# Products of the identity in TensorE's waits in both passes of the first layer's experts

## The chip, the cores and the metric

The kernel runs on one core of a Trainium2 chip. The metric is the device time of one execution in microseconds (us); lower is better. Before the change it is 2140.37 us, the median of three runs (2134.65 to 2141.48).

## What is computed

Two transformer layers, one after the other. The stage that is changed is the mixture of experts of the first layer. Each of 4096 rows of 128 numbers is given to two of eight experts, one after the other, and an expert is two small matrix products with a bias each and a relu between:

```
_L0_ffn_ref(x, gate_W, gate_b, W1, b1, W2, b2, ln_gamma, ln_beta):      # E = 8, D = 128, H = 256, TOP_K = 2
    topk_vals, topk_idx = top_k(softmax(x @ gate_W + gate_b), 2)
    boost = x
    for i in range(2):
        h  = relu(boost @ W1[e] + b1[e])          # e = topk_idx[:, :, i], 128 -> 256
        eo = h @ W2[e] + b2[e]                    # 256 -> 128
        outs.append(eo)
        if i < 1: boost = boost + 0.5 * eo
    fused = sum(topk_vals[:, :, i] * outs[i])
    return layer_norm(x + fused)
```

The rest (an attention before it; behind it a layer that trains its own weights by two gradient steps, and a second mixture of experts) is not touched.

## The kernel before

The stages run one after the other on the five engines; each opens a block of programs, one for each engine, and a barrier stands between the blocks. `experts_0(core, keep, i)` is called twice, for the first (`i = 0`) and for the second expert of each row (`i = 1`); I call the two calls **pass 1** and **pass 2**. Rows have been sorted by expert into 40 tiles of 128 slots (`SLOT_TILES`), so that all rows of a tile have one expert. All programs are written out in full, tile by tile, and run in the order written:

- GpSimd (POOL) gathers the rows of a tile from DRAM into one of eight buffers `xg` (L850). From the ninth tile on it waits for `row_ready`, until the tile that had the buffer before is finished.
- TensorE (PE) takes, in step n, three tiles: it turns the rows of tile n (`turn_rows`, L859), does the first layer of tile n-1 (`first_layer`, L868) and the second of tile n-2 (`second_layer`, L877). A product in float32 takes two instructions on PE, so that the three are 1, 4 and 4 matmul instructions with as many weight loads, 9 a tile.
- ScalarE (ACT) copies the turned rows out of PSUM (`xgT`, L922), does bias and relu of one half of the hidden layer (`hT`, L910) and copies the next tile's weights of the first layer into a ring of three (`own`, L904).
- VectorE (DVE) does the other half of the hidden layer (L934), adds the second bias (`y`, L941) and writes the finished row (L946 to L948), which SyncE (SP) stores to DRAM (L965).

PSUM buffers, `xgT` and `hT` come in pairs, so that PE may write for tile m only when tile m-2 has been read. `keep_busy(pe, bank, ident, n)` puts n products of the identity with itself into a PSUM buffer; nothing reads them. Other stages use it already (30 of them stand ahead of the projections, at 1212 us of the trace); `experts_0` does not.

Of the kernel before, what the change touches and what calls it, by code (L numbers as in the profile page):

```python
# [593 lines left out]
def keep_busy(pe, bank, ident, n):  # L594

    for _ in range(n):
        pe.transpose(bank[:, 0:P], ident[:, :], ident[:, :])
# [210 lines left out]
def experts_0(core, keep, i):  # L808
# [6 lines left out]
    w1, w2, b2, ident = (keep[k] for k in ("w1", "w2", "b2", "ident"))  # L815
# [5 lines left out]
    with ExitStack() as st:  # L821
# [4 lines left out]
        x_ps, y_ps = bank("x_ps"), bank("y_ps")  # L826
        h_ps = [[core.ps(st, f"h_ps{j}_{f}", [P, 512]) for f in range(F)] for j in range(2)]
# [7 lines left out]
        def experts_of(eng, m):  # L835

            _, four = nc.values_load_multi_w_load_instructions(
                expert[0:1, i, m:m + 4], engines=[eng.engine], min_val=0, max_val=E_0 - 1,
                skip_runtime_bounds_check_because="places_0 writes the smaller of a count and E_0 - 1")
            return four  # L840

        @block.gpsimd
        def _(pool):
            if i == 0:
                pool.wait_ge(keep["x_out"], 64)
            for n in range(SLOT_TILES):
                r = n % X_RING
                if n >= X_RING:
                    pool.wait_ge(row_ready, n - X_RING + 1)
                pool.indirect_dma_start(out=xg[r][:, :], out_offset=None, in_=table,  # L850
                                        in_offset=bass.IndirectOffsetOnAxis(ap=source[:, i, n:n + 1], axis=0)).then_inc(gathered[r], 16)

        @block.tensor
        def _(pe):
            def turn_rows(n):
                pe.wait_ge(gathered[n % X_RING], 16 * (n // X_RING + 1))
                if n >= 2:
                    pe.wait_ge(x_ready, n - 1)
                pe.transpose(x_ps[n % 2][:, 0:P], xg[n % X_RING][:, 0:D], ident[:, :]).then_inc(x_turned, 1)  # L859

            def first_layer(m):
                pe.wait_ge(own_ready, m + 1)
                pe.wait_ge(x_ready, m + 1)
                if m >= 2:
                    pe.wait_ge(hT_by_act, m - 1)
                    pe.wait_ge(hT_by_dve, m - 1)
                for f in range(F):
                    mm = pe.matmul(h_ps[m % 2][f][:, 0:P], own[m % W_RING][:, f * P:(f + 1) * P], xgT[m % 2][:, :], start=True, stop=True)  # L868
                mm.then_inc(h_done, 1)

            def second_layer(m, e):
                pe.wait_ge(hT_by_act, m + 1)
                pe.wait_ge(hT_by_dve, m + 1)
                if m >= 2:
                    pe.wait_ge(y_ready, m - 1)
                for f in range(F):
                    mm = pe.matmul(y_ps[m % 2][:, 0:D], hT[m % 2][:, f, :], w2[:, bass.ds(F * e + f, 1), :].rearrange("p a d -> p (a d)"),  # L877
                                   start=(f == 0), stop=(f == F - 1))
                mm.then_inc(y_done, 1)

            if i == 0:
                pe.wait_ge(keep["w_in"], 80)
            for n in range(STEPS):
                if live(n):
                    turn_rows(n)
                if live(n - 1):
                    first_layer(n - 1)
                if live(n - 2):
                    if (n - 2) % 4 == 0:
                        four = experts_of(pe, n - 2)  # L890
                    second_layer(n - 2, four[(n - 2) % 4])
# [1824 lines left out]
```

## Time and profile before

| | |
|---|---|
| median of three runs (not profiled) | 2140.37 us (2134.65 to 2141.48) |
| span of the profiled execution, the only time shown for it | 2178.4 us |
| pass 1 / pass 2 in the trace | 1034 to 1115 us / 1118.5 to 1191.5 us |
| TensorE busy over the span | 1866.1 us (86%) |
| mean granted TensorE clock over the span | 0.921 |

The trace counts time from the first instruction. A row of the timeline has a start, a duration, the engine, the line of the code, the operation with its output and inputs, how many instructions were merged into it, and in brackets how long the engine stood idle before it and what ended that. The granted clock is a share of full speed: 1.00 is 2.4 GHz and 0.50 is 1.2 GHz.

### The profile page before, as it was taken

How to read it: one execution, taken by the hardware profiler on the slowest of the kernel's cores; microseconds unless marked ns; L12 is line 12 of the kernel's file. 1: busy time of each engine (PE TensorE's matmuls, PEld its weight loads, DVE VectorE, ACT ScalarE, POOL GpSimd, SP SyncE). 2: the span in 40 equal slices, each digit the busy share in tenths (PEclk: the TensorE clock that was granted, in tenths of full speed). 3: DMA queues.
4: the chain of work that ended last, by engine and by line, in shares of the span. 5: the costliest groups of instructions: out<-in, count | busy, mean ns of one | idle time of the engine just before them, and what ended most of it. 6: DMA issues, size and time to landing. Idle time of an engine off the chain costs nothing. (4 is left out here: it accounts for less than half of the span.)

```text
span 2178.4 us, 35417 instructions
## 1 busy us (share of the span) xinstructions
PE 1866.1 (86%) x11556; PEld 1497.2 (69%) x11556; DVE 1597.3 (73%) x4179; ACT 1237.1 (57%) x2908; POOL 543.2 (25%) x602
## 2 busy tenths in 40 slices
PE   8999999999999999984766486999889998962772
PEld 6888888888888888873656344777667766741662
DVE  7999999999999999976546475777467765767524
ACT  6888888888888888864444363333233322440333
POOL 0111111111111111110544502444034421000472
PEclk9999999999999999996879587999999999985796
DMA  7000000000000000013554100000000000022354
GB/s 226 1 1 1 1 1 1 1 1 1 1 1 1 1 1 1 1 36 56 99 95 105 52 1 1 0 0 0 1 0 0 0 0 5 2 58 87 85 99 92
DMA packets 64893, 61.06 MB, mean 28 GB/s; under 512 B 10698, under 2 KB 54708, under 8 KB 64612
## 3 DMA queue, kind: packets, MB, share of 16 engines
q1 hardware_dynamic: 52276, 41.50, 6.5%
q0 software_dynamic: 10384, 16.59, 4.9%
q8 instruction: 82, 1.34, 0.3%
q10 hardware_dynamic: 2080, 1.05, 0.2%
q14 instruction: 71, 0.58, 0.1%
HBM read 40.12 MB, written 18.73 MB: 27 GB/s over the span
## 5 line engine op out<-in xcount | busy, mean ns | idle before, releaser
L461 DVE TENSOR_TENSOR probT<-turn_ps,probT 128x512 fp32r<-128x512 f32 x512 | 335.3, 686 | 63.3 <-ACT probT L359 63.2
L374 ACT ACTIVATE prob<-prob,negmax 128x512 f32<-128x512 f32 x512 | 375.4, 740 | 4.6 <-DVE negmax L455 4.6
L176 POOL TENSOR_TENSOR x<-x,scaled 128x512 f32<-128x512 f32 x128 | 166.8, 1303 | 802.1 <-DVE scaled L476 802.1
L455 DVE CUSTOM_DVE_ANT_0 prob<-score_ps,bias 128x512 f32<-128x512 f32 x512 | 341.2, 685 | 6.9 <-issue 1.1
L359 ACT CAST probT<-turn_ps 128x512 fp32r<-128x512 f32 x512 | 284.0, 598 | 21.7 <-PE turn_ps L259 21.7
L259 PE MATMUL turn_ps<-ident,prob 128*128 128x128 f32 x2048 | 266.2, 273 | 1.3 <-DVE probT L461 1.1
L276 PE MATMUL work_ps<-probT,val 128*128 128x512 f32 x1024 | 257.2, 393 | 0.1
L259 PEld LDWEIGHTS turn_ps<-ident,prob 128*128 128x128 f32 x2048 | 236.7, 140 | 28.2 <-DVE probT L461 3.4
L247 PE MATMUL score_ps<-k,q 64*128 64x512 f32 x1536 | 213.8, 410 | 2.4 <-DVE negmax L455 2.1
L276 PEld LDWEIGHTS work_ps<-probT,val 128*128 128x128 f32 x1024 | 187.5, 188 | 39.9 <-DVE probT L461 1.7
L247 PEld LDWEIGHTS score_ps<-k,q 64*128 64x128 f32 x1536 | 135.4, 185 | 47.3 <-issue 19.7
L1587 ACT CAST dpT_hi<-pred_ps 128x128 fp32r<-128x128 f32 x64 | 17.1, 267 | 234.1 <-PE pred_ps L1534 234.1
L291 PE MATMUL work_ps<-wo,ctxT 128*128 128x128 f32 x1024 | 146.0, 286 | 0.7 <-ACT ctxT L366 0.7
L291 PEld LDWEIGHTS work_ps<-wo,ctxT 128*128 128x128 f32 x1024 | 123.9, 191 | 26.3 <-issue 22.6
L1515 POOL TENSOR_TENSOR w<-c,vc 128x512 f32<-128x512 f32 x64 | 83.1, 1298 | 207.1 <-DVE c L1627 207.1
L366 ACT COPY ctxT<-work_ps 128x512 f32<-128x512 f32 x128 | 75.1, 587 | 84.5 <-PE work_ps L276 83.4
L374 ACT ACTIVATION_READ_ACCUMULATOR prob<-prob,negmax 128x1 f32 x512 | 106.1, 207 | 0.0
L476 DVE TENSOR_TENSOR scaled<-work_ps,inv 128x512 f32<-128x512 f32 x128 | 87.8, 686 | 2.7 <-PE work_ps L291 2.7
L1620 DVE TENSOR_TENSOR s<-u_ps,sg 128x512 f32<-128x512 f32 x64 | 44.3, 692 | 54.6 <-ACT sg L1592 54.6
L1504 POOL CAST kTs_hi<-turned_hi 128x128 fp32r (+1 forms) x64 | 45.5, 710 | 133.0 <-SPq L1474 133.0
L868 PE MATMUL h_ps<-xgT,own 128*128 128x128 f32 x320 | 60.6, 320 | 14.5 <-issue 14.5
L877 PE MATMUL y_ps<-w,hT 128*128 x320 | 60.6, 319 | 12.7 <-issue 7.2
(510 smaller groups left out, 4010.5 us busy)
## 6 DMA issues: line engine op xcount, KB each, us to landing
ew<-L_ffn_fc_weight SPq DMA_DIRECT2D x32, 256.0 KB
bias<-bias_line SPq DMA_DIRECT2D x16, 448.0 KB, 8.4
mid_rows<-row SPq DMA_DIRECT2D x40, 128.5 KB
last_rows<-row SPq DMA_DIRECT2D x40, 64.0 KB
rows_dram<-qk SPq DMA_DIRECT2D x1, 2304.0 KB, 18.5
x_rows<-x SPq DMA_DIRECT2D x4, 512.0 KB, 7.1
acc_dram<-zero POOLq DMA_DIRECT2D x1, 2048.0 KB, 16.3
out<-x SPq DMA_DIRECT2D x4, 512.0 KB
```

The costliest lines, as they stand in the source:

```text
L176: pool.tensor_tensor(mine, mine, scaled[a][:, :, :], ALU.add).then_inc(added, 1)
L247: mm = pe.matmul(score_ps[i % 2][a][:, :], q[p % 2][u][head(a), tile_of(i)], k[p % 2][v][head(a), :], start=(n == 0), stop=(n == 2))
L259: mm = pe.transpose(turn_ps[g % 2][:, tile_of(t)], prob[p % 2][a][:, t, tile_of(c)], ident[:, :])
L276: mm = pe.matmul(work[a][:, :], val[p // 2 % 2][:, c, p % 2 * 2 + a, :], probT[n][:, c, :], start=(c == 0 and n == 0), stop=(c == QT - 1 a ...
L291: mm = pe.matmul(work[1][:, tile_of(t)], ctxT[a][:, tile_of(t)], wo[:, 2 * (p % PAIRS) + a, :], start=True, stop=True)
L359: act.copy(probT[0][:, g % QT, :], turn_ps[g % 2][:, :]).then_inc(turned_hi, 1)
L366: act.copy(ctxT[a][:, :], work[a][:, :]).then_inc(ctx_ready, 1)
L374: act.activation(mine, mine, ACT.Exp, bias=negmax[p % 2][:, i, a:a + 1], scale=-1.0, accum_out=total[p % 4][:, i, a:a + 1]).then_inc(exp_d ...
L455: dve.tensor_tensor_reduce(prob[p % 2][a][:, i, :], score_ps[i % 2][a][:, :], bias[:, h, first:first + SEQ][:, ::-1], -1.0, 3.0e38, ALU.ad ...
L461: dve.tensor_tensor(probT[1][:, g % QT, :], turn_ps[g % 2][:, :], probT[0][:, g % QT, :].bitcast(F32), ALU.subtract).then_inc(turned_lo, 1)
L476: dve.tensor_tensor(scaled[a][:, :, :], work[1][:, :].rearrange("p (t d) -> p t d", t=QT), inv[p % 4][:, :, a:a + 1].to_broadcast([P, QT, ...
L1515: pool.tensor_tensor(w[r][:, :], c1[p][:, :], vc[p][:, :], ALU.mult).then_inc(w_ready, 1)
```

## The change

Three edits, all in the program of TensorE in `experts_0`: 24 products of the identity at the start of each pass, two ahead of each first layer and two ahead of each second layer. The two products write into the PSUM buffer that the layer behind them writes. For that the wait until the buffer has been read (`hT_by_act`, `hT_by_dve` of tile m-2, and `y_ready` of tile m-2) stands ahead of the products, and the wait for the operands stands behind them.

```
@@ -859,20 +859,22 @@
             def first_layer(m):
-                pe.wait_ge(own_ready, m + 1)
-                pe.wait_ge(x_ready, m + 1)
                 if m >= 2:
                     pe.wait_ge(hT_by_act, m - 1)
                     pe.wait_ge(hT_by_dve, m - 1)
+                keep_busy(pe, h_ps[m % 2][0], ident, 2)
+                pe.wait_ge(own_ready, m + 1)
+                pe.wait_ge(x_ready, m + 1)
                 for f in range(F):
                     mm = pe.matmul(h_ps[m % 2][f][:, 0:P], own[m % W_RING][:, f * P:(f + 1) * P], xgT[m % 2][:, :], start=True, stop=True)
                 mm.then_inc(h_done, 1)
 
             def second_layer(m, e):
+                if m >= 2:
+                    pe.wait_ge(y_ready, m - 1)
+                keep_busy(pe, y_ps[m % 2], ident, 2)
                 pe.wait_ge(hT_by_act, m + 1)
                 pe.wait_ge(hT_by_dve, m + 1)
-                if m >= 2:
-                    pe.wait_ge(y_ready, m - 1)
                 for f in range(F):
...
@@ -880,6 +882,7 @@
             if i == 0:
                 pe.wait_ge(keep["w_in"], 80)
+            keep_busy(pe, y_ps[0], ident, 24)
             for n in range(STEPS):
```

How TensorE's program starts in pass 1, as a difference; L597 is the product in `keep_busy`, L869 is the L868 of before, `xg_222` the first gathered tile:

```order
 L680 UNCONDITIONAL_BRANCH
 L853 UNCONDITIONAL_BRANCH
+L597 MATMUL y_ps_245<-ident 128x128 x24
 L859 MATMUL x_ps_243<-ident,xg_222 128x128
 L859 MATMUL x_ps_244<-ident,xg_223 128x128
-L868 MATMUL h_ps_0_247<-xgT_237,own_234 128x128
-L868 MATMUL h_ps_1_248<-xgT_237,own_234 128x128
+L597 MATMUL h_ps_0_247<-ident 128x128 x2
+L869 MATMUL h_ps_0_247<-xgT_237,own_234 128x128
+L869 MATMUL h_ps_1_248<-xgT_237,own_234 128x128
```

The 24 products stand ahead of the turn of the first tile. One step in the steady part of pass 1 (turn of the sixth tile, first layer of the fifth, second of the fourth), with its waits, on TensorE before. In the names of the semaphores, `bias_in0_91` is `x_ready`, `bias_in1_92` `own_ready`, `bias_in3_94` and `bias_in4_95` are `hT_by_act` and `hT_by_dve`, and `bias_in6_97` is `y_ready`:

```order
L859 MATMUL x_ps_244<-ident,xg_227 128x128 [waits bias_in0_91,gathered5_265]
L868 MATMUL h_ps_0_247<-xgT_237,own_235 128x128 [waits bias_in3_94,bias_in4_95,bias_in0_91,bias_in1_92]
L868 MATMUL h_ps_1_248<-xgT_237,own_235 128x128
L877 ISA [waits bias_in6_97,bias_in4_95,bias_in3_94]
L877 MATMUL y_ps_246<-w_114,hT_240 128x128
L877 ISA
L877 MATMUL y_ps_246<-w_114,hT_240 128x128
```

and the same step after the change:

```order
L859 MATMUL x_ps_244<-ident,xg_227 128x128 [waits bias_in0_91,gathered5_265]
L597 MATMUL h_ps_0_247<-ident 128x128 [waits bias_in4_95,bias_in3_94]
L597 MATMUL h_ps_0_247<-ident 128x128
L869 MATMUL h_ps_0_247<-xgT_237,own_235 128x128 [waits bias_in0_91,bias_in1_92]
L869 MATMUL h_ps_1_248<-xgT_237,own_235 128x128
L597 MATMUL y_ps_246<-ident 128x128 [waits bias_in6_97]
L597 MATMUL y_ps_246<-ident 128x128
L879 ISA [waits bias_in4_95,bias_in3_94]
L879 MATMUL y_ps_246<-w_114,hT_240 128x128
L879 ISA
L879 MATMUL y_ps_246<-w_114,hT_240 128x128
```

Each layer has two products ahead of it, and the waits are shared out between the products and the layer. The other engines' programs stay as they are.

## Rows read from the trace of the kernel before

**Rows 1.** The page: span, and granted clock of TensorE in 40 slices, in tenths

```profile
span 2178.4 us, 35417 instructions
PEclk9999999999999999996879587999999999985796
```

**Rows 2.** Windows: stretch and length, busy us and instructions by engine, clock, DMA share, GB/s

```profile
1034.00:1115.00 81.00, 60.70 (x360) 54.22 (x360) 46.31 (x200) 36.90 (x120) 38.03 (x40) 0.81 0.60 96
1118.50:1191.50 73.00, 53.86 (x360) 48.25 (x360) 37.22 (x120) 36.42 (x120) 37.91 (x40) 0.88 0.44 108
...
1183.00:1190.00 7.00, 6.59 (x55) 6.15 (x53) 5.78 (x21) 4.56 (x16) 0.95 (x1) 1.00 0.40 84
1107.50:1112.40 4.90, 4.74 (x22) 4.75 (x23) 2.44 (x11) 1.27 (x4) 0.00 (x0) 0.50 0.43 137
```

**Rows 3.** Timeline, TensorE at the end of pass 2: two turns, one tile apart

```profile
1183.98 0.27 PE L859 MATMUL x_ps<-ident,xg 128*128 128x128 f32 x1
...
1184.98 0.27 PE L859 MATMUL x_ps<-ident,xg 128*128 128x128 f32 x1
```

**Rows 4.** Timeline, TensorE early in pass 1: two turns, one tile apart

```profile
1041.73 0.42 PE L859 MATMUL x_ps<-ident,xg 128*128 128x128 f32 x1
...
1043.65 0.42 PE L859 MATMUL x_ps<-ident,xg 128*128 128x128 f32 x1
```

**Rows 5.** Timeline, POOL: gathers in pass 2, the last row its last gather

```profile
1170.73 0.95 POOL L850 DMA_INDIRECT xg<-mid_rows,source  x1 [1.13 <-DVE row L948]
1171.98 0.94 POOL L850 DMA_INDIRECT xg<-mid_rows,source  x1 [0.30 <-issue]
...
1176.12 0.94 POOL L850 DMA_INDIRECT xg<-mid_rows,source  x1 [1.94 <-DVE row L948]
...
1183.02 0.95 POOL L850 DMA_INDIRECT xg<-mid_rows,source  x1 [2.07 <-DVE row L948]
```

**Rows 6.** Timeline, DVE: second biases of pass 2 (tiles 22, 23, 24, 31 and 40)

```profile
1165.19 0.29 DVE L941 TENSOR_TENSOR y<-y_ps,b 128x128 f32<-128x128 f32 x1 [0.53 <-remote]
...
1166.05 0.28 DVE L941 TENSOR_TENSOR y<-y_ps,b 128x128 f32<-128x128 f32 x1
...
1167.19 0.29 DVE L941 TENSOR_TENSOR y<-y_ps,b 128x128 f32<-128x128 f32 x1 [0.22 <-PE y_ps L877]
...
1179.06 0.29 DVE L941 TENSOR_TENSOR y<-y_ps,b 128x128 f32<-128x128 f32 x1 [0.89 <-PE y_ps L877]
...
1190.77 0.29 DVE L941 TENSOR_TENSOR y<-y_ps,b 128x128 f32<-128x128 f32 x1 [0.43 <-PE y_ps L877]
```

**Rows 7.** Timeline, all engines around 1144 us, weight loads left out

```profile
1142.78 0.27 PE L859 MATMUL x_ps<-ident,xg 128*128 128x128 f32 x1
...
1145.25 0.27 ACT L922 COPY xgT<-x_ps 128x128 f32<-128x128 f32 x1 [1.72 <-PE x_ps L859]
1145.33 0.29 DVE L941 TENSOR_TENSOR y<-y_ps,b 128x128 f32<-128x128 f32 x1 [2.37 <-PE y_ps L877]
...
1145.62 0.35 PE L868 MATMUL h_ps<-xgT,own 128*128 128x128 f32 x1 [1.56 <-issue]
```

**Rows 8.** Timeline, first gather and first turn of pass 1 and of pass 2

```profile
1034.36 1.13 POOL L850 DMA_INDIRECT xg<-x_rows,source  x1 [29.10 <-POOLq L680]
...
1037.19 0.45 PE L859 MATMUL x_ps<-ident,xg 128*128 128x128 f32 x1 [4.63 <-DMA xg<-x_rows,source]
...
1119.10 0.94 POOL L850 DMA_INDIRECT xg<-mid_rows,source  x1 [17.02 <-POOLq L821]
...
1121.90 0.48 PE L859 MATMUL x_ps<-ident,xg 128*128 128x128 f32 x1 [7.81 <-DMA xg<-mid_rows,source]
```

**Rows 9.** Timeline of TensorE and windows where 30 such products stand now

```profile
1212.37 6.29 PE L597 MATMUL qk_ps<-ident 128*128 128x128 f32 x30 [5.03 <-DVE projT L1284]
...
1212.00:1218.00 6.00, 5.63 (x27) 5.66 (x28) 5.25 (x21) 1.25 (x4) 4.56 (x5) 0.50 0.20 49
1218.00:1221.00 3.00, 2.18 (x12) 1.32 (x10) 2.03 (x12) 1.43 (x4) 2.39 (x3) 0.97 0.23 60
```

More of the change, by code:

```diff
@@ L861, in first_layer @@
             def first_layer(m):
-                pe.wait_ge(own_ready, m + 1)
-                pe.wait_ge(x_ready, m + 1)
                 if m >= 2:
@@ L866, in first_layer @@
                     pe.wait_ge(hT_by_dve, m - 1)
+                keep_busy(pe, h_ps[m % 2][0], ident, 2)
+                pe.wait_ge(own_ready, m + 1)
+                pe.wait_ge(x_ready, m + 1)
                 for f in range(F):
@@ L871, in second_layer @@
             def second_layer(m, e):
+                if m >= 2:
+                    pe.wait_ge(y_ready, m - 1)
+                keep_busy(pe, y_ps[m % 2], ident, 2)
                 pe.wait_ge(hT_by_act, m + 1)
                 pe.wait_ge(hT_by_dve, m + 1)
-                if m >= 2:
-                    pe.wait_ge(y_ready, m - 1)
                 for f in range(F):
@@ L882, in _ @@
                 pe.wait_ge(keep["w_in"], 80)
+            keep_busy(pe, y_ps[0], ident, 24)
             for n in range(STEPS):
```

## The prediction

> **What bounds the kernel now.** I read the page first. Its slices show the granted clock of TensorE falling from nine tenths to 6, 8, 7, 9, 5, 8 in the middle of the span, and that is where the changed stage lies [rows 1]. The windows of the two passes give the amount: the mean clock is 0.81 over the 81 us of pass 1 and 0.88 over the 73 us of pass 2 [rows 2]. There are two levels, 1.00 and 0.50, so a mean of 0.81 says that 0.19/0.50 = 38% of the time is at half clock: 30.8 us of pass 1, and 24% or 17.5 us of pass 2. That is all that a warm clock can work on.
>
> Next I read what one tile costs on each engine. At full clock TensorE turns tile after tile exactly 1.00 us apart at the end of pass 2, when no gathers run any more, and it is busy throughout: 9 instructions in 1.00 us, 0.111 us each [rows 3], [rows 2]. At half clock two turns are 1.92 us apart, 0.213 us an instruction [rows 4]. GpSimd starts a gather every 1.25 us when nothing holds it [rows 5]. So at full clock it is not TensorE that should set the pace but GpSimd, by 1.25 against 1.00; at half clock it is TensorE, with 1.92.
>
> The trace is slower than either. From tile 22 to tile 31 of pass 2, at full clock throughout, nine tiles take 1179.06 - 1165.19 = 13.87 us, 1.54 us a tile, and the steps are not even: 0.86 and 1.14 us, then a long one [rows 6]. The long one is a stand-still of three engines at once. Around 1144 us a turn that ended at 1143.05 is taken up by ScalarE only at 1145.25, VectorE starts at 1145.33 after 2.37 us of idling, and TensorE at 1145.62, with no releaser that the profile can name [rows 7]. Such a stand-still comes about every third tile while gathers run. GpSimd then idles too, 1.13 and 1.94 us for a finished row [rows 5]. I can't name its cause. It matters for another reason: the profiled span is 2178.4 us and the median run 2140.4, so 38 us of this trace aren't in the timed runs. If both passes had gone at GpSimd's pace, pass 1 would end at 1034.36 + 39 x 1.25 + 7.8 = 1090.9 us (7.8 us is the way from the last gather to the last second bias in pass 2, 1183.02 to 1190.77, [rows 8, 5, 6]) in place of 1115, and pass 2 at 1119.10 + 48.8 + 7.8 = 1175.7 in place of 1191.5: 24 + 16 = 40 us less. This agrees with the 38, so the stand-stills may be the profiler's own. It is an argument, not proof, and I work out both readings.
>
> **The change part by part.** It removes nothing. It adds 2 x 24 + 2 x 40 x 4 = 368 products of the identity, each with its weight load, and puts the waits for free buffers ahead of the waits for operands. Moving the waits alone costs nothing: both sets had to be met before the layer, and they still must. No DMA, no other engine's program and no semaphore is touched; what is queued behind a product is TensorE's own next layer and turn, and behind those ScalarE and VectorE.
>
> *The price of a product.* Like a turn it is one load and one matmul with 128 columns, 0.111 us at full and 0.213 at half clock [rows 3, 4]. The 30 products that stand elsewhere took 6.29 us, most of them at half clock, 0.21 us each [rows 9]. That is the same.
>
> *The start of a pass.* 24 x 0.213 = 5.1 us from the moment at which the pass begins, which I put at GpSimd's first gather: until 1039.5 in pass 1 and 1124.2 in pass 2. The first rows are there at 1037.19 and 1121.90 [rows 8]. The turn is late by 2.3 us in each pass, 4.6 together; if TensorE starts half a microsecond sooner, 3.6.
>
> *The clock.* Do such products raise it? The 30 products begin at half clock with the engine idle for 5.03 us before, and nothing else runs on TensorE beside them; the window to 1218 shows 0.50, the one behind it 0.97 [rows 9]. So they do, and 24 of them should bring full clock at or soon after the first turn. With them TensorE also has little idle time left, so I expect it to stay.
> The Trainium skill speaks against this: its page "TensorE: Matmul & The Clock Gate", part 4, says that full clock does not engage for transpose mode, which is not counted as work. By that rule no clock would be gained and the sum would be that of the fourth case below; the rows just named disagree.
>
> *The pace.* With four products a tile TensorE needs 13 x 0.111 = 1.44 us at full clock. That is above GpSimd's 1.25, above the fast steps of 0.86 to 1.14, and below 1.92. What that is worth depends on the reading.
>
> Reading 1, the stand-stills are not in the timed runs. The pace goes from GpSimd's 1.25 to TensorE's 1.44. Pass 1 ends at 1039.5 + 40 x 1.44 + 0.9 (last second layer to bias) = 1098.0 against 1090.9, pass 2 at 1182.7 against 1175.7: **+14.1 us**, start included.
>
> Reading 2, they are. Tiles at half clock: (30.8 - 3.2)/1.92 = 14 in pass 1 and (17.5 - 3.4)/1.92 = 7 in pass 2, the idle time before the first turn taken off. 59 tiles are at full clock, of them 8 behind the last gather. The other 51 make 17 groups of three. The two fast steps of a group grow from a mean of 1.00 to 1.44, +0.88. In the long one I let two products vanish in the stand-still and two lie behind it, +0.22 (ends: nothing, and 0.44). Groups: 17 x 1.10 = +18.7. The eight last tiles: 7 x 0.44 = +3.1. Starts: +4.6. Tiles at half clock join the groups, whose pace is then 1.54 + 0.37 = 1.91, so 1.92 becomes 1.91: nothing. Only the four tiles at the end of pass 1, at half clock without gathers [rows 2], gain 4 x 0.48 = -1.9. Sum: **+24.5 us**.
>
> I take a value between them, nearer to the first since it explains the 38 us: +18 us, 2140.4 + 18 = **2158 us**.
>
> **The rivals.**
> *The products vanish in the waits, and the clock brings as much as they cost.* For it: in reading 2 TensorE idles 25% of the passes (60.7 us busy of 81, [rows 2]), and if a stand-still lasts until a fixed event and the ring of eight buffers sets the pace, added work in front of it is free. Against it: the fast steps run with TensorE busy without a gap. It leaves the starts (+4.6), the eight tiles (+3.1) and a third of the half-clock tiles' gain (-7 x 0.38 = -2.7): +5, 2145, within 0.3%.
> *Faster, the clock pays.* If the products are hidden and every tile goes at the full-clock pace of 1.54, then the 21 half-clock tiles alone gain 0.38 each, -8.0. The most is the whole difference of the paces: from the first turn to the end, less about 5 us for one tile's way through the engines, pass 1 takes (1115 - 1037.2 - 5)/39 = 1.87 us a tile and pass 2 (1191.5 - 1121.9 - 5)/39 = 1.66, which at 1.54 gives 39 x (0.33 + 0.12) = -17.6; the starts give back 4.6. That is 2127 us. It decides if the timed runs before hold a pace above 1.44 a tile, which is the point from which four products are cheaper than the half clock. Against it stands the 38 us reading, by which that pace is 1.25.
> *Slower still, the clock isn't held.* If products of the identity don't count, the 21 half-clock tiles take 13 x 0.213 = 2.77 in place of 1.92: +17.9 on top of the groups' cost, 2140 + 24.5 + 17.9 = 2183 us. Against it: rows 9.
>
> **How the numbers follow.** Chances: slower by my sums 0.63, balanced 0.18, faster 0.15, much slower 0.04. My case's own range is 2147 to 2170. For the range I reach down towards the faster case and a little above reading 2: 2131 to 2171, which leaves out the fourth case and about half of the faster one. A measurement of this kernel tells 0.3%, or 6.4 us, from no change. Faster than that: 0.15; within: 0.18; slower: 0.67.
>
> **What would show it.** In the trace after: 24 products at the start of a pass ending about 2 us behind the landing of the first rows; granted clock 1.00 from about 1040 us to the end of pass 1 and likewise in pass 2 (if 0.8 as before, the clock step is wrong); turns 1.44 us apart wherever nothing stands still, 13 instructions between them; GpSimd waiting for rows more often than before. The span of the passes could shrink while the timed runs grow, if the stand-stills are the profiler's: the forecast is of the timed runs. I am wrong if the median run before had TensorE at half clock for long, or if the fast steps stay at 1.0 to 1.2 us, which would say that products cost less than 0.111 us beside real work.

## The result, and the profile after

The changed kernel takes 2143.59 us, the median of 20 runs (2138.71 to 2147.03), against 2136.81 us (2132.53 to 2142.37, 20 runs) for the kernel before on the same chip. The ratio is 1.003, with a 95% interval of 1.0022 to 1.0038: 6.4 us slower, with an interval of 4.7 to 8.1 (the two medians are 6.8 us apart). The sign was forecast, the 18 us were not.

The page of the changed kernel, with the lines that answer to [rows 1] and the row of busy times (engine, busy us, share of the span, instructions):

```profile
span 2142.2 us, 36152 instructions
PE 1870.7 (87%) x11924; PEld 1514.3 (71%) x11924; DVE 1598.8 (75%) x4179; ACT 1237.6 (58%) x2908; POOL 544.1 (25%) x602
PEclk9999999999999999997799798999999999985796
```

TensorE's program has 368 more matmuls than that of before (11556). The profiled execution itself took 2144.22 us, 2.0 us more than its span. By the same 2 us an execution whose span is 2178.4 us takes about 2180 us, which no timed run of the kernel before comes near. I took a second profile of that kernel (first experiment), with a span of 2137.7 us, and compare with that one from here on.

TensorE at the start of pass 1 (start, duration, engine, line, operation, count, idle time before and its releaser) and GpSimd's first gather, which answer to [rows 8]:

```profile
1036.44 4.45 PE L597 MATMUL y_ps<-ident 128*128 128x128 f32 x24 [1.07 <-PEq L680]
1037.18 1.13 POOL L850 DMA_INDIRECT xg<-x_rows,source  x1 [29.10 <-POOLq L680]
1040.73 0.27 PE L859 MATMUL x_ps<-ident,xg 128*128 128x128 f32 x1
```

The 24 products begin 0.74 us before the gather and end at 1040.9, 3.7 us behind its start. The first turn is 3.55 us behind the gather in place of 2.83 [rows 8]. What comes next is quicker, since the clock has risen inside the products. Windows of 6 us, with columns as in [rows 2]:

```profile
1034.00:1040.00 6.00, 4.93 (x39) 4.77 (x37) 1.15 (x6) 0.80 (x2) 2.21 (x3) 0.51 0.05 12
1040.00:1046.00 6.00, 5.45 (x48) 5.03 (x47) 2.08 (x8) 3.34 (x11) 4.61 (x5) 1.00 0.25 56
1052.00:1058.00 6.00, 6.00 (x57) 6.00 (x56) 4.94 (x23) 3.84 (x14) 4.48 (x6) 1.00 0.69 139
1082.00:1088.00 6.00, 6.00 (x57) 6.00 (x56) 4.74 (x21) 4.16 (x14) 4.17 (x5) 1.00 0.87 90
```

The granted clock is 0.51 until 1040 and 1.00 from there on, and in the steady part TensorE has no idle time left: 6.00 of 6.00 us. Two of its turns in that part, and two of GpSimd's gathers:

```profile
1072.83 0.27 PE L859 MATMUL x_ps<-ident,xg 128*128 128x128 f32 x1
...
1074.27 0.27 PE L859 MATMUL x_ps<-ident,xg 128*128 128x128 f32 x1
```

```profile
1072.91 0.94 POOL L850 DMA_INDIRECT xg<-x_rows,source  x1 [0.49 <-DVE row L951]
1074.35 0.94 POOL L850 DMA_INDIRECT xg<-x_rows,source  x1 [0.50 <-DVE row L951]
```

A tile takes 1.44 us, 13 x 0.111, and GpSimd now stands idle half a microsecond ahead of each gather until a row is finished (0.30 us stands there also when it waits for nothing, [rows 5]). So TensorE sets the pace, as forecast. At the end of pass 1 it doesn't:

```profile
1092.85 0.33 PE L859 MATMUL x_ps<-ident,xg 128*128 128x128 f32 x1 [0.76 <-DMA xg<-x_rows,source]
1096.18 0.33 PE L859 MATMUL x_ps<-ident,xg 128*128 128x128 f32 x1 [1.67 <-DMA xg<-x_rows,source]
```

These two turns are 3.33 us apart, and the second waits for a gather to land. The same happens before, and longer. The clock stays at 1.00 through this wait:

```profile
1094.00:1096.00 2.00, 0.51 (x5) 0.32 (x3) 1.07 (x5) 0.66 (x2) 0.00 (x0) 1.00 0.51 66
```

The table gives both passes in the two traces. A pass is counted from its first gather to its last second bias; both kernels have 40 tiles in each.

| | before (second profile) | after |
|---|---|---|
| first gather to first second bias, pass 1 / 2 | 7.74 / 7.59 us | 7.18 / 7.04 us |
| pace of second biases, tiles 1 to 32 of pass 1 | 1.34 us | 1.44 us |
| last eight steps of pass 1 | 16.69 us | 14.71 us |
| pass 1 | 66.05 us | 66.63 us |
| pace of second biases, pass 2 | 1.30 us | 1.45 us |
| pass 2 | 58.19 us | 63.53 us |

Pass 1 grows by 0.6 us and pass 2 by 5.3, together 5.9 us, beside 6.4 timed. (The spans differ by 4.5 us. With the same code, the first gather comes anywhere from 1034 to 1037 us in the traces from here on, and what follows pass 2 takes from 967 to 975 us; in these two traces 974.1 and 970.0. So I use the lengths of the passes.)

### The profile page after: what moved, and what is told of

Its sections match the earlier page's. It is cut to its first block and busy times, and to the rows that moved or that the text cites. A ratio compares the mean times of both kernels' runs of the same rounds, so it can differ in the third digit from the quotient of the medians.

```text
span 2142.2 us, 36152 instructions
## 1 busy us (share of the span) xinstructions
PE 1870.7 (87%) x11924; PEld 1514.3 (71%) x11924; DVE 1598.8 (75%) x4179; ACT 1237.6 (58%) x2908; POOL 544.1 (25%) x602
## 5 line engine op out<-in xcount | busy, mean ns | idle before, releaser
L1558 PEld LDWEIGHTS dwp_ps<-dp,h 128*128 128x128 f32 x512 | 67.1, 191 | 5.5
L1566 PE MATMUL pred_ps<-proj,hT 128*128 128x128 f32 x512 | 67.8, 276 | 1.3 <-ACT hT L1604 1.3
```

## The experiments

Kernels of one set ran on one chip. The median of before is 2140.20 us in the first set (the first four below), 2135.95 us in the second (the next four) and 2140.37 us in the third. "Before" and "after" name the two kernels. Lengths of passes come from the one profiled execution of each kernel, ratios from the timed runs.

**The kernel before, profiled again.** No edit. It asks whether the stand-stills of [rows 7] are in an ordinary execution.

> The kernel before, unchanged, once more, for a second trace of it. The stand-still theory (the stand-stills of the first trace belong to that one execution and not to the kernel) expects no stand-stills, gathers 1.25 us apart, a span of 2132 to 2138 us that lies about 2 us below its own time, and the ratio 1.000. The clock theory (the timed runs, too, go at half clock for long) expects granted clock of about 0.81 and 0.88 in the two passes again and tiles of 1.92 us in the middle of them.

Measured: 2139.72 us, ratio 0.9999 (0.9987 to 1.0011), span 2137.7 us. No stand-still of three engines is left in the passes. GpSimd's gathers run 1.25 us apart through all of pass 2 (1105.45 to 1154.44 us, 40 gathers). The clock is at half only for the first tiles of a pass and in one stretch of pass 1; its mean over the passes is 0.89 and 0.93, where the first trace had 0.81 and 0.88 [rows 2]. Windows:

```profile
1034.00:1040.00 6.00, 2.34 (x9) 1.85 (x10) 0.35 (x1) 1.84 (x6) 4.78 (x5) 0.50 0.21 46
...
1052.00:1058.00 6.00, 6.00 (x48) 5.45 (x47) 5.12 (x23) 4.06 (x14) 4.48 (x6) 1.00 0.83 139
```

```profile
1084.00:1090.00 6.00, 4.04 (x26) 3.37 (x27) 2.25 (x10) 2.54 (x8) 1.39 (x2) 0.96 1.03 67
1090.00:1092.00 2.00, 0.58 (x3) 0.28 (x2) 1.07 (x5) 0.54 (x2) 0.00 (x0) 0.50 0.66 75
```

That stretch is new to me. TensorE works 0.58 of 2 us there, although the last gather was issued at 1085.48. Its turns, and the two of GpSimd's gathers that they belong to (the 37th was issued at 1080.24, the 38th at 1082.26 and the 40th at 1085.48):

```profile
1080.24 0.94 POOL L850 DMA_INDIRECT xg<-x_rows,source  x1 [0.30 <-issue]
1082.26 0.94 POOL L850 DMA_INDIRECT xg<-x_rows,source  x1 [1.08 <-DVE row L948]
...
1085.48 0.94 POOL L850 DMA_INDIRECT xg<-x_rows,source  x1 [1.03 <-DVE row L948]
```

```profile
1085.65 0.33 PE L859 MATMUL x_ps<-ident,xg 128*128 128x128 f32 x1 [0.16 <-DMA xg<-x_rows,source]
1088.79 0.33 PE L859 MATMUL x_ps<-ident,xg 128*128 128x128 f32 x1 [1.80 <-DMA xg<-x_rows,source]
1092.34 0.47 PE L859 MATMUL x_ps<-ident,xg 128*128 128x128 f32 x1 [1.76 <-DMA xg<-x_rows,source]
```

From the gather's issue to its turn it is 4 to 5 us for most of pass 1, then 6.7 us for the 36th, 8.55 for the 37th (1088.79 - 1080.24), and 10.1, 10.9 and 10.8 for the last three. For the 37th and the 38th TensorE stands waiting; the turns of the last two follow 2.05 and 1.92 us apart, at about its pace at half clock. VectorE's rows wait there too, for the stores of earlier rows:

```profile
1090.03 0.29 DVE L946 SCALAR_TENSOR_TENSOR row<-y,xg 128x128 f32<-128x128 f32 x1 [2.54 <-DMA mid_rows<-row]
```

**The parts of the change.** Four kernels, each the changed one with products taken out; the order of the waits stays as changed. Only the 24 at the start:

```
-                keep_busy(pe, h_ps[m % 2][0], ident, 2)
-                keep_busy(pe, y_ps[m % 2], ident, 2)
```

> Only the 24 products at the start of each pass, with the waits in the order of the change; none at the tiles. The pace theory (four products a tile lift TensorE's need from 1.00 to 1.44 us, above GpSimd's 1.25) expects 0 to 4 us less than before, -1 us likeliest: the turn of the first tile 0.7 us late, but the first tiles at full clock. The clock theory expects that the clock falls again later in the passes and the time stays as before within 3 us.

Measured: 2142.94 us, ratio 1.0011 (0.9998 to 1.0023). The first second bias is 7.15 and 6.88 us behind the gather, 0.6 to 0.7 us sooner than before, and the passes aren't shorter (67.39 and 58.43 us): from there GpSimd and the landings set the end. The pace theory's 0 to 4 us less were not measured; the ratio leaves room for 0.4 us less at most.

Only the two and two of each tile:

```
-            keep_busy(pe, y_ps[0], ident, 24)
```

> Only the two and two products at each tile, none at the start. The pace theory expects tiles 1.44 us apart from when the clock is up, and the first two or three at 13 x 0.213 = 2.8 us, so 7 to 12 us more than before, more than the whole change. The clock theory expects the time of the change less at most 2 us.

Measured: 2150.71 us, ratio 1.0048 (1.0031 to 1.0065), passes of 70.81 and 64.03 us. Without the 24, the first tiles carry their products at half clock and the first second bias comes 8.97 and 8.68 us behind the gather. Beside products in every tile, then, the 24 look worth a gain: the whole change is 1.003. The intervals of the two ratios, from two sets of runs, overlap (1.0022 to 1.0038 for the change), but the passes of the change are 4.7 us shorter together.

No products, only the moved waits (all three calls taken out):

> Only the order of the waits of the change, no product at all. Both theories expect the time of before within 1 us (ratio 1.000) and the trace of before. If it differs by 3 us or more, the order of the waits has a price of its own that the prediction set to nothing.

Measured: 2140.73 us, ratio 1.0001 (0.9989 to 1.0013). The order of the waits is worth nothing that could be measured (2.8 us at most).

**More and fewer products in a tile.** The 24 stay. One and one:

```
-                keep_busy(pe, h_ps[m % 2][0], ident, 2)
+                keep_busy(pe, h_ps[m % 2][0], ident, 1)
-                keep_busy(pe, y_ps[m % 2], ident, 2)
+                keep_busy(pe, y_ps[m % 2], ident, 1)
```

> The change with one product ahead of each layer in place of two. The pace theory expects 11 x 0.111 = 1.22 us a tile, still under GpSimd's 1.25, so that the products cost 0 to 2 us over the time of before (ratio 1.000 to 1.001). The theory that every product is paid for (about 6 us for four a tile, so half of that for two) expects 3 us more, ratio 1.0015.

Measured: 2137.14 us, ratio 0.9999 (0.9989 to 1.0008). Turns come every 1.22 us (1070.78, 1072.03 and 1073.25), with longer steps in between, as before (the passes take 66.25 and 57.95 us). TensorE needs 11 x 0.111 = 1.22, less than GpSimd's 1.25: free as far as can be measured.

Four and four, with 4 for 1 in the same lines:

> The change with four products ahead of each layer in place of two. The pace theory expects tiles 17 x 0.111 = 1.89 us apart in both passes: 39 x (1.89 - 1.30) = 23 us more in pass 2 and 31 x (1.89 - 1.34) = 17 us more in the first 32 tiles of pass 1, nothing in its last eight, so 35 to 42 us over before (ratio 1.017 to 1.020). If waits hid products, it would be clearly less, 12 to 20 us.

Measured: 2170.80 us, ratio 1.017 (1.0157 to 1.0183). Turns in the steady part:

```profile
1068.72 0.27 PE L859 MATMUL x_ps<-ident,xg 128*128 128x128 f32 x1
...
1070.59 0.27 PE L859 MATMUL x_ps<-ident,xg 128*128 128x128 f32 x1
...
1072.47 0.27 PE L859 MATMUL x_ps<-ident,xg 128*128 128x128 f32 x1
```

A tile takes 1.87 us; 17 x 0.111 is 1.89. The passes take 79.69 and 79.72 us, that is alike: at this pace the gathers land in time at the end of pass 1 too. Its last eight steps take 13.9 us, 2.8 less than before, where I had expected no difference.

**The late landings at the end of pass 1.** The eight experts' last tiles are filled up: 4096 rows are 32 tiles' worth, the stage has 40, so the last tile at least, and probably several, must be all empty slots. For an empty slot the table of rows holds 0, and its gather fetches row 0. If that one row is the cause, empty slots that fetch different rows should land in time. The edit is in the place where the table is made, on VectorE, some time ahead of the passes; an empty slot of pass 1 now fetches the row whose number is its lane:

```
             for i in range(R):
...
-                then(dve.scalar_tensor_tensor(source[:, i, :], back_ps[i][:, 0, :], float(P), line[i][:, :], ALU.mult, ALU.add))
+                if i == 0:
+                    then(dve.scalar_tensor_tensor(at[:, :], back_ps[i][:, 0, :], float(P), line[i][:, :], ALU.mult, ALU.add))
+                    then(dve.scalar_tensor_tensor(line[i][:, :], at[:, :], 0.0, token_line[:, 0:1].to_broadcast([P, K]), ALU.is_equal, ALU.mult))
+                    then(dve.tensor_tensor(source[:, i, :], at[:, :], line[i][:, :], ALU.add))
```

In the kernel before:

> The kernel before, but the empty slots of pass 1 gather the row of their own lane (0 to 127) and not row 0 all of them; two small VectorE operations more ahead of pass 1 (0.4 us). Theory of the repeated row (the last tiles of pass 1 are slow since the 128 slots of the empty tiles fetch one and the same row) expects the last eight tiles in 9 to 12 us in place of 16.7, landings of 5 us in place of 6 to 11, and 4 to 7 us less than before (ratio 0.997 to 0.998). If the tail has another cause: ratio 1.000 and the tail of 16.7 us again.

Measured: 2131.13 us, ratio 0.9977 (0.9968 to 0.9985), which is faster than both kernels. Pass 1 takes 58.10 us in place of 66.05, its last eight steps 9.51 in place of 16.69, and the last six gathers land in 4.3 to 4.8 us. What the DMA engines did from 1084 to 1096 us, in the kernel before and then in this one (queue, packets, MB, share of 16 engines; then issues, and median us to landing):

```profile
q0 software_dynamic: 129, 0.24, 63.0%
...
xg<-x_rows,source POOLq DMA_INDIRECT x2, 10.1
```

```profile
q0 software_dynamic: 132, 0.27, 19.6%
...
xg<-x_rows,source POOLq DMA_INDIRECT x3, 4.1
```

About the same number of packets of the gathers' queue (q0) takes 63% of the engines' time with one row repeated and 19.6% with different rows. (The windows don't hold the same gathers of pass 1, so this shows a packet's price, not the amount of work.) With the tail mended the clock doesn't fall there either: it is 1.00 in every window from 1084 to 1096 us.

The same edit in the changed kernel:

> The changed kernel with the same spread gathers in pass 1. Theory of the repeated row (a tail that waits for landings took the products' price in pass 1 away): with the tail gone the whole price shows, 8 to 12 us over the before kernel with spread gathers in place of 6, that is about 2 to 5 us over the kernel before (ratio 1.001 to 1.002). If the tail has another cause: 6 us over the before kernel with spread gathers, as without it.

Measured: 2143.06 us, ratio 1.003 (1.0017 to 1.0043). Against the kernel just above, on the same chip, that is 11.9 us. Its passes take 64.60 and 63.05 us. That is within the 8 to 12 us expected, but the changed kernel's own time isn't: 2 to 5 us over before were expected and 6 to 7 measured, so it gains nothing that could be measured from the spread rows (1.003 with and without them, in two sets of runs), where the kernel before gains 4.8 us. In its trace the last eight steps do shrink, from 14.71 to 10.69 us, and three single steps of 2.0 to 2.4 us earlier in pass 1 take about half of that back; the rest is open. Second biases in its tail are 1.44 us apart, TensorE's own pace:

```profile
1093.81 0.29 DVE L950 TENSOR_TENSOR y<-y_ps,b 128x128 f32<-128x128 f32 x1 [0.24 <-PE y_ps L885]
1095.25 0.29 DVE L950 TENSOR_TENSOR y<-y_ps,b 128x128 f32<-128x128 f32 x1 [0.24 <-PE y_ps L885]
```

**One pass alone.** The changed kernel with all its products in one pass only; the other pass has none. The edit for pass 1 (for pass 2 it tests `i == 1`):

```
-                keep_busy(pe, h_ps[m % 2][0], ident, 2)
+                keep_busy(pe, h_ps[m % 2][0], ident, 2 if i == 0 else 0)
-                keep_busy(pe, y_ps[m % 2], ident, 2)
+                keep_busy(pe, y_ps[m % 2], ident, 2 if i == 0 else 0)
-            keep_busy(pe, y_ps[0], ident, 24)
+            keep_busy(pe, y_ps[0], ident, 24 if i == 0 else 0)
```

> All products of the change in pass 1, none in pass 2. By the traces so far (pass 1 took 66.05 us before and 66.63 after, pass 2 took 58.19 and 63.53) it should cost 0 to 2 us over before, ratio 1.000 to 1.001. The theory that each pass bears half of the price expects 3 us, ratio 1.0015.

Measured: 2141.01 us, ratio 1.0007 (0.9995 to 1.0018).

> All products of the change in pass 2, none in pass 1. By the traces so far 5 to 6 us over before, ratio 1.0025. The theory that each pass bears half expects 3 us, ratio 1.0015.

Measured: 2144.85 us, ratio 1.0023 (1.0012 to 1.0034). The two excesses, 0.0007 and 0.0023, add up to that of the change, and it is pass 2 that is measurably slower. The intervals of the two ratios overlap (up to 1.0018, from 1.0012), but on the same chip the medians are 3.8 us apart and the means of the twelve times 3.2, give or take 2.2. In the profiled execution with products in pass 1 alone, that pass takes 68.72 us, more than the timed excess would have it. Its tail begins sooner, with a step of 4.80 us at the 32nd tile, in which VectorE waits 3.71 us for the store of an earlier row:

```profile
1091.25 0.29 DVE L949 SCALAR_TENSOR_TENSOR row<-y,xg 128x128 f32<-128x128 f32 x1 [3.71 <-DMA mid_rows<-row]
```

So the length of the tail differs from one execution to another, and single traces are good for a microsecond or two there: with one row repeated and no products at its tiles, pass 1 takes 66.05, 67.39, 68.08 and 66.28 us in four traces, and with the whole change 66.63 and 68.72. The 0.6 us of the table are one draw from this. Pass 2 is steadier: 57.9 to 58.4 us in five traces without products at its tiles, 63.0 to 63.5 in three with two and two and the 24.

**Spread rows in both passes,** in the kernel before: the edit of above for both passes (`if i < 2`). In pass 2 it can also send the slot of one token, whose true row number is 0, to another row.

> The kernel before with the gathers of the empty slots spread over rows 0 to 127 in both passes. In pass 2 the one token whose row lies in slot 0 may get another token's row; nothing else is changed. If the repeated row also delays the last tiles of pass 2 (landings of 4.6 to 5.7 us there against 3 to 4 before them), it gains 1 to 2 us more than the spread in pass 1 alone, ratio 0.9970; if not, it stays at 0.9977.

Measured: 2130.70 us, ratio 0.9954 (0.9939 to 0.997): the fastest kernel of the study. Pass 1 takes 59.68 us, pass 2 55.77 in place of 58.19, and the last gathers of pass 2 are turned 3.3 to 4.1 us after their issue in place of 4.6 to 5.7. So the repeated row also delays the end of pass 2, by much less. Why less, I haven't tried. The timed gain is larger than I expected (ratio 0.9970) and than the passes show, which together are only 0.8 us shorter than with the spread in pass 1 alone; the intervals of the two ratios touch. And since one token of pass 2 may get another token's row, this kernel is a probe and not a replacement.

## Why the prediction was right in sign and wrong in size

*The price of a product* was right: 0.111 us at full clock. The turns are 1.22, 1.44 and 1.87 us apart with 2, 4 and 8 products in a tile, against 11, 13 and 17 x 0.111.

*The clock* was right in part. It rises inside the 24 products (0.51 until 1040 us) and stays at 1.00 from there to the end of pass 1, the tail included. The Trainium skill's rule on transpose mode ("TensorE: Matmul & The Clock Gate", part 4) would have had it stay at half; these windows disagree (`keep_busy` calls `pe.transpose`). But there was less for it to work on than the 38% and 24% of half clock that I had read from [rows 2]: in the second profile of before only the first four tiles or so of a pass and the stretch from about 1090 to 1096 us are at half clock, and the means of 0.89 and 0.93 make that 22% and 14%.

*The moved waits* cost nothing, as said.

*The choice between the two readings* failed. "I take a value between them, nearer to the first", +18 us, gave weight to a reading in which a tile waits in stand-stills like [rows 7]. The second profile has none, and the paces of the other kernels leave no room for one every third tile; the trace that I worked from was of an execution about 40 us longer than those that were timed. What made it longer stays open. The first reading alone gave +14.1 us. That is still more than twice the 6.4 measured. It was 2 x 63.6 us for the passes after less 56.5 and 56.6 before; the traces have 66.6 and 63.5 after, 66.05 and 58.2 before. So nearly all of its error is that I had the passes before 11.1 us too short together, 9.5 of them in pass 1; pass 1 after, 3.0 us longer than I had it, gives some of that back. Three steps of it were off:

*The start of a pass,* "The turn is late by 2.3 us in each pass, 4.6 together". It had the products begin with the gather and run at half clock throughout. They begin 0.7 us before it and take 4.45 us, not 5.1; the clock is up when they end. Then the first tiles run at full clock, so that the first second bias comes 0.56 and 0.55 us sooner than before, not later. Where tiles carry products of their own, the 24 save what those would cost at half clock (ratio 1.0048 without them, 1.003 with them). That pass 2 after still took the 63.5 us for which I had 63.6 is partly luck: three early steps of 2.05, 1.57 and 1.88 us in place of 1.44 made up for the sooner start.

*Pass 2 before,* "If both passes had gone at GpSimd's pace". In pass 2 GpSimd does issue every 1.25 us to the end, as I had it; what was off is the way from the last gather to the last second bias, 9.2 us (1163.64 - 1154.44), where I had taken 7.8. With it pass 2 before is 58.2 us, not 56.6. After it is 63.5, where I had 63.6. So the products cost 5.3 us there and not 7.1. With the rows spread in pass 2 too, that way is 6.65 us (1157.10 - 1150.45), so the repeated row is in it. The second biases come 1.30 us apart on the mean, among steps of 1.0 to 1.6 us about one in ten of 1.9 to 2.4. In pass 2 these follow turns for which TensorE waits until a gather has landed, as the 14th:

```profile
1125.71 0.33 PE L859 MATMUL x_ps<-ident,xg 128*128 128x128 f32 x1 [1.06 <-DMA xg<-mid_rows,source]
```

They don't hold up GpSimd's gathers. Why those landings are late I haven't tested.

*The end of pass 1.* This is the largest term. I had pass 1 of before end at GpSimd's pace plus 7.8 us, 56.5 us in all, and it takes 66.05. TensorE waits at its last tiles for gathers that land some 10 us after their issue, and slower work ahead of such a wait is hidden in it: after the change pass 1 is 66.6 us, and only 0.6 of my 7.1 us is to be seen in these two traces, and 1.5 us in the timed runs with products in pass 1 alone (ratio 1.0007). The spread rows show this from the other side. With the tail gone, passes before are 58.1 and 58.1 us and the products cost 11.9 us; from the four lengths of the traces it is 11.4. My first reading comes near it once its passes before are set right: 14.1 less twice the 1.6 us by which 58.1 exceeds what I had is 10.9. The clock has a part in this end too. In the wait it falls to 0.50 before (1090 to 1096 us) and stays at 1.00 after, as in the kernels with only the tiles' products and with products in pass 1 alone, so that the last tiles go faster there. What that is worth inside the 16.69 and 14.71 us of the last eight steps I haven't separated. That an end of a pass waits for landings was in the trace of before too, though not among the rows that I built on (the turn at 1105.01 us waits 1.52 us for a gather): I had read the steady part and the last pass, and carried the 7.8 us from there to pass 1.

The rivals: "The products vanish in the waits, and the clock brings as much as they cost" came nearest in size, 2145 us and within 0.3%, but by another way. The waits that hide products are the landings at the end of pass 1, not stand-stills, and the clock's gain is that of the start and, by a part not measured, of the end of pass 1. "Slower still, the clock isn't held" is ruled out by the clock of 0.98 over both passes after. "Faster, the clock pays" asked for a pace before of over 1.44 us; it is 1.30 to 1.34.

Open: the stand-stills of the first profile; the late landings behind the single long steps before; why the changed kernel gains nothing from the spread rows; and how the 10 us of a landing divide between the gather itself and the queue before it.

## What to carry to other kernels

Before working from a trace, lay its span beside the timed runs: here the trace was 38 us too long, and the reading that built on its stand-stills came out at 24.5 us where 6.4 were measured. In this kernel, work put into an engine's waits cost what it exceeded of the slack to the engine that sets the pace: two products a tile, 1.22 of 1.25 us, cost nothing that could be measured, four cost 0.1 to 0.15 us a tile and eight some 0.55. And look at the end of each pass by itself, since work that lies ahead of a late transfer can cost next to nothing until the transfer is mended (6.4 us with the late landings, 11.9 without).

## What the runs showed of the hardware

I hadn't expected that indirect gathers whose empty slots all name one row in DRAM are so slow: 8.6 to 10.9 us from issue to use at the end of pass 1, with a median landing of 10.1 us for the last two, against 4.3 to 4.8 us for the same gathers with different rows (landing 4.1), and three times the DMA engines' time for as many packets. How many of the 128 slots of each were empty I haven't read. Spreading them over 128 rows is what made this kernel faster, to ratios of 0.9977 (pass 1) and 0.9954 (both passes, with the reservation made there), where the products made it slower.
